# A state-space layer with an attention and expert layer on one core: the start of the expert part and the last layer norm rewritten

## The reference, cut to what matters

```python
x = layernorm(x + mamba(x))                 # selective scan, 512 channels, 16 states
# second layer:
q, k, v = project(rmsnorm(x, ln1_w))        # 16 heads of 128
hid = x + softmax(causal(q k^T)) v @ o_w.T
x2 = rmsnorm(hid, ln2_w)
logits = x2 @ gate_w.T                      # 16 experts
probs = softmax(logits); top_w, top_i = top_k(probs, 4); top_w /= sum(top_w)
wfull = scatter of top_w over the 16 experts
routed = sum_e wfull[t, e] * (silu(g_e) * u_e) @ w2_e.T     # every expert for every token
shared = silu(x2 @ sg.T) * (x2 @ su.T) @ sh_down.T
x = layernorm(x + (hid + routed + shared))
```

## Time and profile before

| what | value |
|---|---|
| median of 3 runs (lowest, highest) | 842.04 us (841.83, 843.49) |
| the profiled execution's own time | 840.52 us |
| its span, first to last instruction | 838.7 us |
| granted TensorE clock, mean | 0.974 of full speed |
| busy: PE, DVE, ACT, POOL | 753.9, 612.3, 452.2, 326.1 us |
| attention ends (last matmul of `last_outputs`) | at 595.6 us |
| first gate/up matmul of the experts | at 608.15 us |
| groups 1, 2, 3 of the experts | 42.0, 41.9, 41.9 us each |

### The profile page before, as it was taken

The page is one execution under the profiler, slowest core; times in us unless marked ns, Lnnn a source line. Parts: engine busy times, 40 slices in busy tenths (PEclk is TensorE's granted clock), DMA queues, the critical chain, the costliest instruction groups (busy, mean ns, idle before and its releaser), DMA issues. The chain is left out here.

```text
span 838.7 us, 11966 instructions
## 1 busy us (share of the span) xinstructions
PE 753.9 (90%) x3972; PEld 562.7 (67%) x3972; DVE 612.3 (73%) x1235; ACT 452.2 (54%) x953; POOL 326.1 (39%) x183
## 2 busy tenths in 40 slices
PE   6985788788869999999999999997788999999996
PEld 2432233334424689898898889987566889898985
DVE  3688999999998777857874776686475373737376
ACT  3696655666646266736763774576543252525151
POOL 9007999898868731111120211112252030303030
PEclk9996999999999999999999999999889999999999
DMA  8000000000000301000010010000125452525201
GB/s 295 20 1 1 0 1 0 0 1 0 0 1 0 102 1 51 26 27 26 27 41 11 25 50 26 20 20 20 57 75 132 142 161 60 157 62 160 59 0 50
DMA packets 14458, 39.98 MB, mean 48 GB/s; under 512 B 2368, under 2 KB 3904, under 8 KB 14288
## 3 DMA queue, kind: packets, MB, share of 16 engines
q1 hardware_dynamic: 14416, 39.46, 15.5%
HBM read 38.34 MB, written 1.11 MB: 47 GB/s over the span
## 5 line engine op out<-in xcount | busy, mean ns | idle before, releaser
L307 POOL TENSOR_TENSOR m_ring<-m_du,m_b_sb 128x1024 f32<-128x1024 f32 x64 | 149.6, 2358 | 66.7 <-DVE m_du L703 46.2
L730 DVE TENSOR_TENSOR_SCAN m_ring<-ps,m_ring 128x1024 f32<-128x1024 f32 x64 | 145.3, 2281 | 4.5 <-POOL m_ring L307 2.8
L998 POOL TENSOR_TENSOR a_wl<-raw,a_wh 128x1024 fp32r<-128x1024 f32 x16 | 39.9, 2496 | 246.2 <-ACT a_wh L1184 246.2
L420 PE MATMUL ps<-m_ring,ident 128*128 128x512 f32 x256 | 128.7, 618 | 0.0
L1505 POOL TENSOR_TENSOR e_wl<-raw,e_wh 128x512 fp32r<-128x512 f32 (+1 forms) x55 | 57.3, 1047 | 161.0 <-ACT e_wh L1610 85.8
L599 ACT ACTIVATE ps<-m_delta,m_negA 128x510 f32<-128x510 f32 x128 | 82.6, 682 | 6.3 <-DVE m_ring L730 4.2
L854 PE MATMUL ps<-e_rms_hi,e_wh 128*128 128x512 f32 x200 | 79.7, 398 | 4.7 <-ACT e_sg L1623 3.2
L420 PEld LDWEIGHTS ps<-m_ring,ident 128*128 128x128 f32 x256 | 50.8, 199 | 43.7 <-issue 41.0
L855 PE MATMUL ps<-e_rms_lo,e_wh 128*128 128x512 f32 x200 | 79.6, 398 | 0.0
L856 PE MATMUL ps<-e_rms_hi,e_wl 128*128 128x512 f32 x200 | 79.3, 396 | 0.0
L550 ACT ACTIVATE m_b_sb<-ps 128x512 f32<-128x512 f32 x64 | 38.0, 594 | 64.2 <-PE ps L364 64.1
(11 more groups left out here) (198 smaller groups left out, 2052.6 us busy)
## 6 DMA issues: line engine op xcount, KB each, us to landing
raw<-in_expert_w SPq DMA_DIRECT2D x30, 384.0 KB, 3.5
raw<-in_attn_w SPq DMA_DIRECT2D x20, 512.0 KB, 3.3
e_wb<-wt SPq DMA_DIRECT2D x20, 256.0 KB, 4.5
e_wb<-wt SPq DMA_DIRECT2D x4, 448.0 KB, 5.7
e_wb<-wt SPq DMA_DIRECT2D x4, 384.0 KB, 4.6
e_wb<-wt SPq DMA_DIRECT2D x4, 320.0 KB, 4.6
m_first<-in_xT SPq DMA_DIRECT2D x2, 512.0 KB, 5.5
x<-in_x_tok SPq DMA_DIRECT2D x1, 1024.0 KB, 10.3
```

What stands on the lines that cost most here:

```text
L307: nc.gpsimd.tensor_tensor(split(slot(n)), du[:, pair_of(ph):pair_of(ph) + 2, halves(ph)], b_sb[:, n % B_BUFS:n % B_BUFS + 1, :].to_broadca ...
L420: nc.tensor.matmul(ps[:, Y_BANK + c, :], ident[:, :], slot(n)[:, c * HALF:(c + 1) * HALF], start=False, stop=False, skip_group_check=True) ...
L730: nc.vector.tensor_tensor_scan(slot(n), dA_of(n), slot(n), 0.0, ALU.mult, ALU.add).then_inc(scan_done, 1)
L998: nc.gpsimd.tensor_tensor(w[1][:, j, :], raw[:, j, :], w[0][:, j, :].bitcast(F32), ALU.subtract).then_inc(w_done, 1)
```

## The change

The arithmetic of the result stays; only the inverse root of the RMS norm gets another first value (exp(-0.5 ln) in place of the reciprocal of a square root), refined by the same Newton step.

1. **One Block.** The expert part's lists are appended to those of scan and attention; the barrier is gone. Its buffers are laid over attention buffers that are free by then, and the high and low parts of x2 reuse the attention's `rows`. ACT waits for the last scores (`scores_over`) before it writes expert weights.
2. **Roots by halves.** Sums, squares, root, Newton step, row scaling, transposes and the splits run for tiles 0 to 3, then 4 to 7. The root is Ln and then Exp on ACT. PE computes half 1's transposes between tile 0's two `gate_up` calls.
3. **Token-major logits.** For each of 8 tiles 6 matmuls with 128 columns of weights (the tokens) and 16 columns of data (the gate); the copy L1665 and the transposes L1556 go.
4. **Routing in one piece**, behind the product of tile 0's first half; PE turns the weights after tile 1 instead of 2. POOL's `hid += x1` waits for the routing weights.
5. **Attention's last slab** is rounded by ACT at the start of the last step instead of ahead of its last instruction.
6. **Last layer norm** in three parts: tiles 0 to 3, 4 and 5, 6 and 7.

```diff
             if not units:
+                pack(j, g * 16 + 32)
                 high_p(n, 0)
                 exps(n + 2, 2)
...
                 high_o(n + 2, j, 2)
-                pack(j, g * 16 + 32)
                 high_o(n + 3, j, 3)
...
-        nc.scalar.preload_act_table_set("sqrt_and_others")
-        squares(nc, act, keep, lambda i: hid[:, i, :], lambda i: v[0][:, 0, i, :],
-                lambda i: act.wait_ge(r_free, out_unit(NG - 1, i) + 1), sq_done, root)
...
+        scores_over(act)
+        for k in range(SH_TILES):
+            high_w(k, 16)
+        for i in range(TT // 2):
+            squares(i)
+        roots(0)
+        for k in range(SH_TILES, GM):
+            high_w(k, 16)
+        squares(4)
+        squares(5)
+        for c in range(DC):
+            high_x(0, c)
+        squares(6)
+        squares(7)
+        roots(1)
+        nc.scalar.preload_act_table_set("silu_and_others")
...
+        def roots(half):
+            of = stats[:, tiles_of(half), :]
+            act.wait_ge(sq_done, (half + 1) * TT // 2)
+            nc.scalar.activation(of[:, :, 2], of[:, :, 0], ACT.Ln, scale=1.0 / D, bias=keep["eps"][:, 1:2]
+                                 ).then_inc(log_done, 1)
+            act.wait_ge(log_done, half + 1)
+            nc.scalar.activation(of[:, :, 3], of[:, :, 2], ACT.Exp, scale=-0.5).then_inc(root, 1)
...
-            pool.wait_ge(xn_done, 2 * DC)
+        pool.wait_ge(wf_done, 1)
             nc.gpsimd.tensor_tensor(hid[:], hid[:], x1[:], ALU.add).then_inc(x_added, 1)
...
+        def logits(half):
+            if half == 0:
+                pe.wait_ge(gl_done, 1)
+            pe.wait_ge(xn_done, 2 * half + 2)
+            for i in range(half * TT // 2, (half + 1) * TT // 2):
+                for c in range(DC):
+                    mm = three_passes(nc, ps[:, 6, i * NE:(i + 1) * NE], [x[:, c, i * P:(i + 1) * P] for x in xn],
+                                      [x[:, c, :] for x in gate], c == 0, c == DC - 1)
+            mm.then_inc(lg_ready, 1)
...
+                gate_up(g, k, 0)
+                if first and k == 0:
+                    turn(1)
+                    logits(1)
+                gate_up(g, k, 1)
+                if first and k == 1:
+                    turn_weights()
...
+        turn(0)
+        logits(0)
+        summed(pe, TT - 1)
+        group(0)
...
+        for i in range(TT // 2):
+            last_sum(dve, i)
+        mean_squares(0)
+        scale_rows(0)
+        for i in range(TT // 2, TT):
+            last_sum(dve, i)
+        for c in range(DC):
+            low_x(0, c)
+        mean_squares(1)
+        scale_rows(1)
+        for c in range(DC):
+            low_x(1, c)
+        tiles(0)
...
-    LN_PARTS = 2
+    LN_PARTS = ((0, 4), (4, 6), (6, 8))
```

More of the change, by code:

```diff
@@ L856, in three_passes @@
     return nc.tensor.matmul(out, ll, rh, start=False, stop=stop, skip_group_check=True)
-def squares(nc, act, keep, src, junk, wait, sq_done, root):
-    stats = keep["stats"]
-    for i in range(TT):
-        wait(i)
-        nc.scalar.activation(junk(i), src(i), ACT.Square, accum_out=stats[:, i, 0:1]).then_inc(sq_done, 1)
-    act.wait_ge(sq_done, TT)
-    nc.scalar.activation(stats[:, :, 2], stats[:, :, 0], ACT.Sqrt, scale=1.0 / D,
-                         bias=keep["eps"][:, 1:2]).then_inc(root, 1)
@@ L1328, in add_output @@
                 dve.wait_ge(r_ready, out_unit(g, i) + 1)
[L1329 to L1331 removed]
+                nc.vector.tensor_tensor(hid[:, i, :], hid[:, i, :], ring(i)[:, 0:D], ALU.add).then_inc(r_free, 1)
         def first(s):
@@ new lines, in expert_block, with tiles_of, halves, turn_bank @@
+    LN_PARTS = ((0, 4), (4, 6), (6, 8))
+    def tiles_of(half):
+        return slice(half * TT // 2, (half + 1) * TT // 2)
+    def halves(half):
+        return slice(half * HALF, (half + 1) * HALF)
+    def turn_bank(half, c):
+        return ps[:, 2 + 2 * half + c, :]
+    DOWN_AT = [[k] for k in range(GM - 2)] + [[GM - 2, GM - 1], []]
+    def sync(sp):
+        def load(g, j):
+            sp.wait_ge(w_done, g * GM + (j + 1 - GM))
+            sp.dma_start(raw[:, j, 0:FPACK], d["expert_w"][g * GM + j]).then_inc(ld_w[j], 16)
+        def spread(g, k):
+            row = (g * GM + k - SH_TILES) * P
+            cut = min(EI - row % EI, P)
+            cut = P // 2 if cut == P else cut
+            if g > (k < SH_TILES):
+                sp.wait_ge(aw_done, 2 * ((g - 1) * GM + k + 1))
+            for lo, hi in ((0, cut), (cut, P)):
+                e = (row + lo) // EI
+                sp.dma_start(wb[lo:hi, k, :], wt_dram[e:e + 1, :].to_broadcast([hi - lo, T])
+                             ).then_inc(ld_wb[k], 16)
+        for j in range(GM):
+            load(1, j)
+        sp.wait_ge(wT_done, 1)
+        sp.dma_start(wt_dram, wT[:]).then_inc(wt_stored, 16)
+        sp.wait_ge(wt_stored, 16)
+        for k in range(SH_TILES, GM):
+            spread(0, k)
+        for k in range(SH_TILES):
+            spread(1, k)
+        for g in range(2, NMG + 1):
+            for j in range(GM):
+                load(g, j)
+                if g > 2 or j >= SH_TILES:
+                    spread(g - 1, j)
+        for i in range(TT):
+            sp.wait_ge(ln, i + 1)
+            sp.dma_start(out[:, i, :], hid[:, i, :]).then_inc(stored, 16)
+        sp.wait_ge(stored, 16 * TT)
@@ new lines, in gpsimd, with rest @@
+    def gpsimd(pool):
+        pool.wait_ge(gh_done, 1)
+        nc.gpsimd.tensor_tensor(gate[1][:], gate_raw[:], gate[0][:].bitcast(F32), ALU.subtract).then_inc(gl_done, 1)
+        def rest(j, k, cols, high, low):
+            pool.wait_ge(high, j + 1)
+            nc.gpsimd.tensor_tensor(w[1][:, k, cols], raw[:, k, cols], w[0][:, k, cols].bitcast(F32),
+                                    ALU.subtract).then_inc(low, 1)
+        for k in range(GM):
+            rest(k, k, slice(0, 2 * D), wh_done, w_done)
+        pool.wait_ge(wf_done, 1)
+        nc.gpsimd.tensor_tensor(hid[:], hid[:], x1[:], ALU.add).then_inc(x_added, 1)
+        with pool.Fori(0, NMG) as g:
+            for k in range(GM):
+                for kd in DOWN_AT[k]:
+                    rest(g * GM + kd, kd, slice(2 * D, 3 * D), dh_done, d_done)
+                rest(g * GM + (k + GM), k, slice(0, 2 * D), wh_done, w_done)
@@ L1785, in constants @@
     }
[L1786 removed]
+    for name in ("ld_small", "wh_done", "w_done", "hid_ready", "x_kept"):
         keep[name] = ctx.enter_context(nc.semaphore(name))
@@ L1813, in program @@
             scan = mamba_block(nc, part, d, keep, ps, space, rows)
-            attention = attention_block(nc, part, d, keep, ps, space, rows)
+            attention, after = attention_block(nc, part, d, keep, ps, space, rows)
+            experts = expert_block(nc, part, d, keep, ps, space, (rows.hi, rows.lo), after, out)
             with nc.Block() as block:
@@ L1839, in _ @@
                     attention[4](dve)
-        with ExitStack() as part:
-            expert_block(nc, part, d, keep, ps, out)
+                    experts[4](dve)
 def layouts(i):
```

588 lines of the change are left out of this document (261 added, 327 removed).

## The result

| | before | changed kernel |
|---|---|---|
| median (lowest, highest) of 15 runs | 842.13 us (840.04, 844.57) | 837.96 us (834.06, 841.00) |
| ratio to before, 95% interval | | 0.9955 (0.9940 to 0.9971) |
| the profiled execution's own time, span | 840.52, 838.7 us | 834.06, 832.3 us |
| first gate/up matmul | 608.15 | 604.61 |
| group 1 begins | 662.52 | 658.08 |

What follows compares the result with a forecast made beforehand. PE, waiting at times, was taken to bound the stretch before group 1, slowed by lower clock and DVE-POOL blocking. -8.4 to group 1, +3.4 clock, -0.3 tail made -5.3: 836.7 us, range 830.0 to 841.5.

Steps and rivals of the forecast that it cites:

- step C: First gate/up matmul to group 1: routing weights at 616.4 instead of 630.71; group 1 -8.4 us, Step B included, before clock.
- Step A: Attention's last slab rounded early: PE's 2.18 us wait goes, POOL blocks DVE, outputs +0.35 us; +2.6 more with slow clock.
- I charge a slow phase: PE's 3.0 us idle gap ahead of half 0's logits lowers the clock: +3.4 us, bounds 0 and +6.8.
- Step B: Attention outputs' end to half 0's first gate/up matmul: 602.5 instead of 608.15, -5.65 us; 24 logits matmuls take 2.2.
- Step D: Tail behind the last product: last layer norm part scales two tiles instead of four, -0.3 us (-0.6 to +0.5).
- The slow clock comes twice: Rival: a second slow phase, in the attention's outputs or behind tile 0, gives 839 to 841 us; chance 0.22 excluded, 0.17.
- the forecast case: One slow phase ahead of the logits: 836.7 us, own range 834.5 to 838.5; chance 0.48.
- No blocking: Rival: POOL does not block DVE at the new pairs (L1309, Newton step, `low`): -15.9 us, 826.1; chance 0.06.
- PE never settles: Rival: at the first gate/up calls waits keep PE's clock low, +13.7 us of slow work: 844.7 us; chance 0.07.

Runs made afterwards that it cites:

- e3: Changed kernel with POOL's residual sum released by the last scaled row and the routing cut in three pieces again: 841.29 us, ratio 1.0008 to the kernel before.
- e1: Changed kernel with the attention's last slab rounded at its old place again: 835.15 us, ratio 0.9921 to the kernel before.
- e6: Changed kernel with e1's and e2's edits and PE's gaps filled with 14, 18 and 12 transposes: 830.05 us, ratio 0.9844 to the kernel before.
- e12: Changed kernel with old slab place, early residual sum, late weight rounding, logits between gate/up matmuls, and gaps filled with wide matmuls: 830.54 us, ratio 0.9864 to before.
- e8: Kernel before with only the early rounding of the attention's last slab: 842.11 us, ratio 0.9993 to the kernel before.
- e9: Changed kernel with its two gaps ahead of the logits filled by 10 and 6 matmuls of 512 columns: 833.91 us, ratio 0.9908 to before.
- e10: e9 with each half's logits matmuls set between tile 0's gate/up matmuls: 836.55 us, ratio 0.9931 to the kernel before.
- e2: Changed kernel with POOL's residual sum released by the last scaled row instead of the routing weights: 838.13 us, ratio 0.9945 to the kernel before.
- e11: Changed kernel with every logits matmul issued twice: 848.63 us, ratio 1.0081 to the kernel before.
- e4: Changed kernel with the last layer norm in two parts of four tiles: 838.23 us, ratio 0.9968 to the kernel before.
- e5: Changed kernel with its two gaps ahead of the logits filled by 18 and 12 transposes of 128 columns: 833.89 us, ratio 0.9895 to before.
- e7: Changed kernel with weight tiles 3 and 4 rounded behind the second root instead of the first: 836.19 us, ratio 0.9915 to the kernel before.

## Why the prediction was right, and where its steps were not

**Sign and size.** 836.7 was forecast and 837.96 measured; the interval of the ratio gives 837.1 to 839.7 from 842.13. The ratio is clear of no change, and the measured median lies in the forecast's own range of 834.5 to 838.5. The closeness is in part luck. In the pair of profiles group 1 was forecast at 657.5 and came at 658.1, but as a sum of errors: the outputs started 1.9 us late, of which 0.4 was there before the step; each logits block took 0.5 more; and PE's waits in step C were 2.7 shorter (1.78, 0.74 and 0.75 instead of 2.2, 2.3 and 1.5). Behind group 1 the profile gained 2.0 us instead of 0.3, and the median gives 2.3 us of the profile's gain back, with a lower mean clock.

**Step C held.** The chain took 5.77 (5.75 forecast). The residual sum blocked the low pair by 4.4 (3.9). With the slow phase of 3.4 added, the routing weights were due at 619.8 and came at 620.3, the copy at 629.0 and came at 629.55, the first routed product at 637.6 and came at 637.7, group 1 at 657.5 and came at 658.1. That the gain hangs on this step is what e3 shows. The wait of 2.3 for the bank was 0.74, and those at `down` 0.75 and 0.72 instead of 1.5 and 1.1. A likely reason is that PE came later than forecast (its first gate/up matmul at 604.6 instead of 602.5), so that DVE's delay hurt less; no run isolates it.

**Step A failed in size.** "+0.35" stood where the profiles have 1.9 us, counted from the step's first transposes (15.19 to the outputs, 13.31 before). The blocking was there, and so was the lower clock in the last step, from 576.66 to 583.49, which the prediction had only as a bound (+2.6) and in the rival "twice". But the 1.9 isn't all the early slab's. The clock fell 0.6 us into PE's wait of 2.51, and it fell in the last step of e1, e6 and e12 as well, which have the slab at its old place and a wait of 1.14; it then lasted 3.4 us, and e1's outputs started at 14.57. So between e1 and the changed kernel the slab itself is 0.6, and the other 1.3 is a clock that fell in these executions and not in the one profiled of the kernel before. Why is open. In the whole time e1 supports the sign; e8 doesn't.

**The clock: right sum in the middle, incomplete cause.** The 3.4 us between 596 and 650 came as 1.7 + 1.7, behind the two blocks of logits. The step that failed is "I charge a slow phase" for the idle gap, with nothing for the logits: in the profiled execution the first 21 logits matmuls behind the gap ran at the upper level and the clock fell at 603.97, inside unbroken work, and with the gap filled it fell all the same (e9); with the logits spread it didn't (e10). The gap matters too: where it isn't filled, the level can fall inside it, ahead of the logits (601.06 in e2, 601.02 in e11), and the phases last longer. Whether the gap had a part in the fall at 603.97 no run tells.

**Step B** was 0.5 us short for a logits block: 0.111 us each, 24 in 2.7 instead of 2.2, the upper end of the bound. That agrees with the Trainium skill's figure in "TensorE: Matmul & The Clock Gate", section "LDWEIGHTS (loading the stationary operand)", of about 107 ns for 128 columns. The spacing of 0.06, which pulled the estimate down, is not what this form has.

**Step D** gave 0.6 in the profile (0.3 forecast), 0.5 against e4's; too little for the medians.

**Not in the prediction:** 1.3 us in groups 1 to 3, in which it said that nothing changes; see the last section.

**The rivals.** "The slow clock comes twice" (839 to 841) has in its span, or at its edge, seven of the 15 executions of the changed kernel, and the forecast case, with its own range of 834.5 to 838.5, seven others; the median is one of these. The shortest execution does have the lower clock in the last step as well as behind the logits, as that rival says, and still took 834.06. The chances of 0.48 and 0.17 should have been nearer to each other. "No blocking" is refuted by four rows (1.70, 1.30, 1.22, 5.86). "PE never settles" did not come; e11, with 13.7 and 10.2 us at the lower level and 848.6 us, is the nearest to it.

## What to carry to other kernels

A matmul with 16 columns of data cost 0.11 us here and, in an unbroken row of 24, the clock of the work behind it. Put between wide ones, such matmuls kept the clock (e10), but look at what then comes later: here it was the routing, and the time was no better. Filling PE's waits of 2.62 and 1.78 us with work into a free bank was worth 4 to 5 us by the ratios. When an operation of POOL is given a new place, look which DVE operations with both operands in on-chip memory, or scalings there, run beside it, and put it where DVE waits for PE (here behind the last scaled row: 5.86 became 1.48 us). Where executions fall into groups by their mean clock, compare them at like clock too: e2's median shows nothing, its executions at like clock do.

## What the runs showed of the hardware that was not expected

- A row of 24 matmuls with 16 columns was enough to bring PE to its lower level (602.88 and 613.12 in e9, whose gaps were filled; 621.5 in e11, inside the row), and 48 of them in a row at the lower level ran for 10.2 us without its coming back. Behind them matmuls with 512 columns ran at the lower level for another 2.8 us in the changed kernel (604.61 to 607.4), but for 5.3 in e4's (604.70 to 609.97). The Trainium skill's page "TensorE: Matmul & The Clock Gate" says in its Part 1 that the clock follows how busy PE has been recently; here the clock fell behind rows in which PE had a matmul every 0.11 us, with a wait of 0.32 us ahead of them in e9.
- The executions of one kernel on the same inputs fall into groups (834, 837.5, 840.7 us) with the mean clock.
- The loops of groups 1 to 3 have the same instructions in both kernels, and PE is at 1.00 in both. Yet gate/up matmuls stood 0.229 us apart on average before and 0.227 after, in every one of the three groups, which makes 0.2 us a group; e8, derived from the kernel before, has 0.229 too, and e5 and e11, derived from the changed one, 0.227. The rest is in `down`, and goes both ways: single groups take 0.4 us longer there, two of three before (42.2), one in e8 (42.2, 41.8, 41.8), none in the changed kernel's profile, but two in e11 (42.0, 42.0, 41.6) and one in e5, e7 and e12. Where the buffers lie is one thing that differs between the two kernels. No run moved a buffer alone, so the cause stays open.
- Open as well: why the clock falls in the attention's last step in every profile but that of the kernel before, and why e8's local loss of 1.9 us is not in its median.
